# The modulated layer inside the recurrence's loop: four steps at a time, one body behind

## The reference

```python
x = x + lstm(x, h0=cond, Wx, Wh, b)      # x: (2, 1024, 256), cond: (2, 256)
x = x + modulated(x, cond, weight)       # weight: (256, 256)

def step(carry, xw_t):                   # 1024 times, one behind the other
    prev_h, prev_c = carry
    a = xw_t + prev_h @ Wh               # four gates of 256
    i, f, o = sigmoid(a[:, :256]), sigmoid(a[:, 256:512]), sigmoid(a[:, 512:768])
    g = tanh(a[:, 768:])
    next_c = f * prev_c + i * g
    next_h = o * tanh(next_c)
    return ((next_h, next_c), next_h)

ys = y * (1 / sqrt(256))                 # y: cond
d = rsqrt(einsum('bi,io->bo', ys * ys, weight * weight) + 1e-8)
out = einsum('bsi,io->bso', x * ys[:, None, :], weight) * d[:, None, :]
```

## Time and profile before

| | us |
|---|---|
| median of 3 runs | 1782.44 (1782.1 to 1782.82) |
| the profiled execution | 1781.28 |
| its span, first to last instruction | 1779.5 |
| PE busy | 1674.8 (94%) |
| PE weight loads busy | 1618.9 (91%) |
| ACT busy | 1096.3 (62%) |
| DVE busy | 1001.7 (56%) |
| POOL busy | 259.7 (15%) |
| mean granted TensorE clock | 0.993 of full |

### The profile page before, as it was taken

The page is one execution under the profiler, slowest core; times in us unless marked ns, Lnnn a source line. Parts: engine busy times, 40 slices in busy tenths (PEclk is TensorE's granted clock), DMA queues, the critical chain, the costliest instruction groups (busy, mean ns, idle before and its releaser), DMA issues.

```text
span 1779.5 us, 356718 instructions
## 1 busy us (share of the span) xinstructions
PE 1674.8 (94%) x164620; PEld 1618.9 (91%) x164620; DVE 1001.7 (56%) x7455; ACT 1096.3 (62%) x8196; POOL 259.7 (15%) x1293
## 2 busy tenths in 40 slices
PE   7999999999999999999999999999999999999998
PEld 6999999999999999999999999999999999999996
DVE  2555555555555555555555555555555555555554
ACT  2666666666666666666666666666666666666663
POOL 0111111111111111111111111111111111111110
PEclk7999999999999999999999999999999999999999
DMA  2000000000000000000000000000000000000001
GB/s 78 26 0 0 0 0 0 0 0 0 0 0 0 0 0 0 0 0 0 0 0 0 0 0 0 0 0 0 0 0 0 0 0 0 0 0 0 0 0 47
DMA packets 4585, 6.69 MB, mean 4 GB/s; under 512 B 1248, under 2 KB 3040, under 8 KB 4576
## 3 DMA queue, kind: packets, MB, share of 16 engines
q1 hardware_dynamic: 3872, 5.51, 0.9%
q10 hardware_dynamic: 704, 1.05, 0.2%
HBM read 4.46 MB, written 2.10 MB: 4 GB/s over the span
## 4 chain that ended last, share of the span: by engine, by line
PE 82%; DVE 12%; ACT 3%; issue 2%; DMA 0%; SPq 0%; POOL 0%; DVEq 0%
PE pG L228 32%; PE pX L210 18%; PE pH L228 14%; PE pS L228 14%; DVE pH L373 4%; DVE pH L349 4%; PE pF L241 3%; ACT fgate L186 3%; DVE hst L380 2%; DVE parts L368 2%; DVE pG L345 1%; PE pG L310 1%; DMA xh<-in_xT_dram 0%; PE pS L301 0%; DVE ores L397 0%
## 5 line engine op out<-in xcount | busy, mean ns | idle before, releaser
L228 PE MATMUL pG<-hst,wh_sb 128*32 128x16 f32 x65536 | 1081.6, 187 | 89.0 <-DVE hst L380 87.8
L228 PEld LDWEIGHTS pG<-hst,wh_sb 128*32 128x32 f32 x65536 | 943.4, 109 | 136.9 <-DVE hst L380 112.6
L186 ACT ACTIVATE fgate<-pH 128x2 f32<-128x2 f32 x2048 | 353.9, 173 | 601.0 <-PE pH L228 600.6
L228 PE MATMUL pH<-hst,wh_sb 128*32 128x16 f32 x32768 | 673.4, 185 | 3.5 <-issue 3.5
L368 DVE TENSOR_TENSOR parts<-fgate,pH 128x2 f32<-128x2 f32 x2048 | 320.3, 156 | 583.6 <-ACT fgate L186 583.4
L228 PEld LDWEIGHTS pH<-hst,wh_sb 128*32 128x32 f32 x32768 | 589.0, 110 | 2.1 <-issue 2.1
L228 PE MATMUL pS<-hst,wh_sb 128*32 128x16 f32 x32768 | 506.8, 186 | 3.4 <-issue 3.4
L210 PE MATMUL pX<-xp,wx_sb 128*32 128x8 f32 x32896 | 459.6, 181 | 2.9 <-issue 1.8
L228 PEld LDWEIGHTS pS<-hst,wh_sb 128*32 128x32 f32 x32768 | 424.4, 108 | 3.6 <-issue 3.6
L147 POOL TENSOR_TENSOR xh<-xh,hst 128x4 f32 (+1 forms) x1024 | 208.7, 204 | 1490.3 <-DVE hst L380 1490.3
L373 DVE TENSOR_TENSOR_SCAN pH<-parts 128x6 f32<-128x6 f32 x2048 | 367.2, 179 | 82.9 <-ACT parts L188 0.9
(11 more groups left out here) (41 smaller groups left out, 179.4 us busy)
## 6 DMA issues: line engine op xcount, KB each, us to landing
outT_dram<-ores SPq DMA_DIRECT2D x8, 256.0 KB, 2.5
xh<-in_xT_dram SPq DMA_DIRECT2D x6, 320.0 KB
wh_sb<-in_Wh_dram ACTq DMA_DIRECT2D x1, 1024.0 KB, 7.9
wx_sb<-in_Wx_dram SPq DMA_DIRECT2D x1, 1024.0 KB, 7.4
w_sb<-in_w_dram SPq DMA_DIRECT2D x1, 256.0 KB, 6.2
xh<-in_xT_dram SPq DMA_DIRECT2D x2, 64.0 KB, 8.0
condT<-in_condT_dram ACTq DMA_DIRECT2D x1, 2.0 KB, 7.6
bias_col<-in_bC_dram ACTq DMA_DIRECT2D x1, 3.0 KB, 7.3
```

The lines of the kernel that those rows point to most:

```text
L186: act.activation(fgate[:, j, :], forgets[j][:, cols], ACT.Sigmoid).then_inc(fgate_ready[j], 1)
L228: last = pe.matmul(to[c * Q:(c + 1) * Q, :], tile(wh_sb[:, k, :], c, j, g), hst[:, k, WIDE * t:WIDE * (t + 1)], start=False, stop=True, sk ...
```

## The change

The layer moves into the loop, one body behind the recurrence.

- POOL, once a body and behind the spread of x: `xm` = the body's four positions of `xh` times `yscale` (one buffer), and `res` += `xh` for the four positions that DVE has scaled. In front stand waits for its own adds, for PE's last layer sums (the buffer `xm` is read by them), and for DVE's last scaling. POOL also loads w itself, at the begin, and squares it in one instruction before the second spread.
- PE, in step 3 behind the output gate's matmuls: 16 matmuls (32 passes) of `w_sb` with `xm` into `pL`, a bank of its own in place of the filler's. The filler now goes into unused columns of the bank pX and stands before step 2's sums of x, not behind them.
- DVE, in step 0 between the multiply and the scan of half 0: `res` = `pL` times `demod`, at an address that depends on the counter.
- Before the loop: the sums for d on PE in 16 matmuls of 32 columns behind the warming ones and before the first sums of x, + eps on DVE, square root on ACT (its table is loaded first, the sigmoid's after it), reciprocal on DVE.
- SP sends `res` in three pieces, positions 0 to 511, 512 to 959, 960 to 1023, two DMAs each. All the work behind the loop but two scalings, two adds and one set of 16 matmuls is gone. `xh` and `res` begin with 8 columns of padding (X0), so that the first two sets, which hold nothing, have a place.

```diff
-    FILL = (0, 0, 1, 0)
+    X0 = 2 * T
+        xm = sb("xm", [P, K, ROWS])
+        res = sb("res", [P, K, B, X0 + SEQ])
-        wmod = sb("wmod", [P, B, K, D])
-        ores = sb("ores", [P, 2, NOUT])
-        pF = ctx.enter_context(nc.psum_tensor("pF", [P, 512], F32))
+        pL = ctx.enter_context(nc.psum_tensor("pL", [P, 512], F32))
...
+        OUTCUT = [0, 512, 960, SEQ]
@@ sync
+            for lo, hi in zip(OUTCUT, OUTCUT[1:]):
+                sp.wait_ge(result_ready, hi // T + 2)
+                for o in range(K):
+                    sp.dma_start(outT[o * P:(o + 1) * P, :, lo:hi], res[:, o, :, X0 + lo:X0 + hi]).then_inc(out_written, 16)
@@ gpsimd
+            pool.dma_start(w_sb[:, :, :], w.rearrange("(k p) o -> p k o", p=P)).then_inc(w_loaded, 16)
...
+            def add_x(n):
+                cols = bass.ds(n * T, T) if not isinstance(n, int) else slice(n * T, (n + 1) * T)
+                pool.tensor_tensor(res[:, :, :, cols], res[:, :, :, cols], xh[:, :, :, cols], ALU.add).then_inc(result_ready, 1)
             pool.wait_ge(x_begun, 16 * K)
-            spread(slice(0, T))
+            spread(slice(X0, X0 + T))
+            pool.wait_ge(w_loaded, 16)
+            pool.tensor_tensor(wsq[:, :, :], w_sb[:, :, :], w_sb[:, :, :], ALU.mult).then_inc(squares_ready, 1)
...
+                    pool.wait_ge(xh_ready, it * T + 2 * T)
+                    pool.wait_ge(layer_summed, it + 2)
+                    pool.wait_ge(layer_scaled, it + 1)
                     pool.wait_ge(x_summed, it + 2)
-                    spread(bass.ds(it * T + 2 * T, T))
+                    spread(bass.ds(it * T + (X0 + 2 * T), T))
+                    pool.tensor_tensor(xm[:, :, :].rearrange("p k (b t) -> p k b t", b=B), xh[:, :, :, bass.ds(it * T + X0, T)],
+                                       yscale[:, :, :].unsqueeze(3).broadcast_to([P, K, B, T]), ALU.mult).then_inc(xm_ready, 1)
+                    add_x(it)
@@ scalar
+            act.activation(warmed[:, 0:1], zeros[:, 0:1], ACT.Sqrt)
+            act.wait_ge(demod_added, 1)
+            act.activation(demod[:, :, :], demod[:, :, :], ACT.Sqrt).then_inc(demod_rooted, 1)
+            act.activation(warmed[:, 1:2], zeros[:, 0:1], ACT.Sigmoid)
@@ tensor
+            def sum_layer():
+                for o in range(K):
+                    for k in range(K):
+                        for c in range(G):
+                            lo = o * P + c * Q
+                            last = pe.matmul(layer[c * Q:(c + 1) * Q, o * ROWS:(o + 1) * ROWS], w_sb[:, k, lo:lo + Q], xm[:, k, :],
+                                             start=(o == 0 and k == 0), stop=True, skip_group_check=True)
+                return last
...
                     elif s == 2:
+                        filler(1)
                         sum_x_outs().then_inc(x_summed, 1)
                     else:
                         pe.wait_ge(xh_ready, it * T + (2 * T - 1))
-                    filler(FILL[s])
+                        pe.wait_ge(xm_ready, it + 1)
+                        sum_layer().then_inc(layer_summed, 1)
@@ vector
+            def scale_layer(n):
+                cols = bass.ds(n * T, T) if not isinstance(n, int) else slice(n * T, (n + 1) * T)
+                dve.wait_ge(layer_summed, n + 1)
+                dve.tensor_tensor(res[:, :, :, cols], layer.rearrange("p (o b t) -> p o b t", o=K, b=B),
+                                  demod[:, :, :].unsqueeze(3).broadcast_to([P, K, B, T]), ALU.mult).then_inc(layer_scaled, 1)
...
                         if s == T - 1:
                             carry_forget(j)
+                        elif s == 0 and j == 0:
+                            scale_layer(it)
                         dve.wait_ge(parts_ready[j], it * (2 * T) + 2 * (s + 1))
```

More of the change, by code:

```diff
@@ L52, in build @@
         zeros = sb("zeros", [P, P])
-        warmed = sb("warmed", [P, 1])
+        warmed = sb("warmed", [P, 2])
         condT = sb("condT", [P, K, B])
@@ L118, in _ @@
                 for k in range(K):
[L119 to L126, removed]
+                    sp.dma_start(xh[:, k, :, X0 + lo:X0 + hi], xT_in[k * P:(k + 1) * P, :, lo:hi]).then_inc(x_loaded, 16)
@@ L162, in _ @@
             pool.wait_ge(x_loaded, 16 * K * (len(XCUT) - 2))
[L163 to L169, removed]
+            bodies(EARLY, NBODY)
+            for n in (NBODY, NBODY + 1):
+                pool.wait_ge(layer_scaled, n + 1)
+                add_x(n)
         @block.scalar
@@ L236, in clear @@
                 for c in range(G):
-                    pe.matmul(of[c * Q:(c + 1) * Q, :], picks[:, :], zeros[:, 0:of.shape[1]], start=True, stop=True)
+                    last = pe.matmul(of[c * Q:(c + 1) * Q, :], picks[:, :], zeros[:, 0:of.shape[1]], start=True, stop=True)
+                return last
[6 more added lines that the diff above has]
+                                             start=(o == 0 and k == 0), stop=True, skip_group_check=True)
+                return last
             def filler(count, start=False):
                 for _ in range(count):
-                    pe.matmul(pF[0:Q, 0:P], picks[:, :], zeros[:, :], start=start, stop=True, skip_group_check=True)
+                    pe.matmul(pX[0:Q, 256:256 + P], picks[:, :], zeros[:, :], start=start, stop=True, skip_group_check=True)
             pe.wait_ge(zeros_ready, 1)
@@ L249, in _ @@
                 clear(outs[j])
+            clear(layer).then_inc(layer_summed, 1)
             filler(WARM, True)
+            pe.wait_ge(squares_ready, 1)
+            pe.wait_ge(ysq_ready, 1)
+            for o in range(K):
+                for k in range(K):
+                    for c in range(G):
+                        lo = o * P + c * Q
+                        last = pe.matmul(squared[c * Q:(c + 1) * Q, o * B:(o + 1) * B], wsq[:, k, lo:lo + Q], ysq[:, k, :],
+                                         start=(o == 0 and k == 0), stop=True, skip_group_check=True)
+            last.then_inc(demod_summed, 1)
             pe.wait_ge(operands_ready, 2)
@@ L293, in _ @@
                         pe.wait_ge(xh_ready, it * T + (2 * T - 1))
-                    filler(FILL[s])
-            pe.wait_ge(squares_ready, K)
-            pe.wait_ge(outs_carried, NBODY + 1)
-            pe.wait_ge(h_ready[0], SEQ + 1)
-            for o in range(K):
-                for k in range(K):
-                    last = pe.matmul(pD[:, o * B:(o + 1) * B], wsq[:, k, o * P:(o + 1) * P], ysq[:, k, :],
-                                     start=(k == 0), stop=(k == K - 1))
-            last.then_inc(demod_summed, 1)
-            pe.wait_ge(wmod_ready, B * K)
-            pe.wait_ge(xh_ready, T + SEQ)
-            for n, (b, ch, o) in enumerate(UNITS):
-                if n >= 2:
-                    pe.wait_ge(result_ready, n - 1)
-                for k in range(K):
-                    last = pe.matmul(pO[n % 2][:, :], wmod[:, b, k, o * P:(o + 1) * P],
-                                     xh[:, k, b, ch * NOUT:(ch + 1) * NOUT], start=(k == 0), stop=(k == K - 1))
-                last.then_inc(layer_summed, 1)
+                        pe.wait_ge(xm_ready, it + 1)
+                        sum_layer().then_inc(layer_summed, 1)
+            pe.wait_ge(layer_scaled, NBODY + 1)
+            pe.wait_ge(xm_ready, NBODY + 1)
+            sum_layer().then_inc(layer_summed, 1)
         @block.vector
@@ L342, in _ @@
                 dve.tensor_copy(hst[:, j, h_slot(0):h_slot(0) + B], condT[:, j, :]).then_inc(h_ready[j], 1)
+            dve.wait_ge(demod_summed, 1)
+            dve.tensor_scalar(demod[:, :, :], squared.rearrange("p (o b) -> p o b", o=K), EPS, None, ALU.add).then_inc(demod_added, 1)
             def carry_pair(j):
@@ L384, in _ @@
                         carry_outs()
[L386 to L399 removed]
+            for n in (NBODY, NBODY + 1):
+                scale_layer(n)
 def kernel(**inputs):
```

62 lines of the change are left out of this document (23 added, 39 removed).

## The result

| | before | after |
|---|---|---|
| median of the runs, us | 1782.56 (1782.1 to 1782.82) | 1852.34 (1850.8 to 1852.49) |
| span of the profiled execution, us | 1779.5 | 1850.5 |
| mean granted TensorE clock | 0.993 | 0.994 |
| PE busy | 94% | 97% |

What follows compares the result with a forecast made beforehand. The recurrence PE to ScalarE to VectorE and back was taken as the bound. About 0.32 us per body times 256 is 81; 1781.3 + 81 + 2 - 13.3 = 1851, median 1852, range 1806 to 1888.

Steps and rivals of the forecast that it cites:

- PE's step 3: Loop's end on PE: the layer's 32 passes and waits delay the branch and next body by 0.22 us per body.
- the room: PE's back edge: of 0.44 us idle, the branch needs 0.34 to 0.39, leaving 0.05 to 0.10 free.
- DVE's step 0: Between multiply and first scan: scaling's register instructions delay the scan 0.10 us per body (0.04 to 0.18, or nothing).
- PE's step 2: Filler moves ahead of the output gate's sums of x; last load comes 0 to 0.03 us late, 0.01 taken.
- start: Before the loop: loading and squaring w and PE's demodulation passes, partly offset by earlier instruction stops, add 2 us (0 to 4).
- tail: From the last h to the end: 5.5 us instead of 18.8, a gain of 13.3 us.
- body: One loop pass of four steps: about 7.1 us expected, against 6.76 before.
- the 1.2 added for the median: Whole kernel: median of the runs lies 1.2 us above the profiled execution, taking 1851 to 1852.
- The rival in which PE's sequencer hides the branch by running ahead of the array: PE's back edge: sequencer over about 0.25 us ahead, both prices hidden, kernel faster at 1771 us; chance 0.09.
- One sign of being right: Step 3's end: some 0.3 us idle between last pL load and next body's first load, put down to issue, not h.
- The late copy: POOL's copy of x for PE comes some 0.35 us later; hidden, but up to 0.05 per body without the late edge.

Runs made afterwards that it cites:

- 32 dummy passes: Kernel before plus 16 matmuls (32 passes of zeros into a spare bank) at the end of step 3: 1832.27 us, ratio 1.029.
- 8 passes: Kernel before plus 4 matmuls (8 passes of zeros into a spare bank) at the end of step 3: 1781.64 us, ratio 0.9997.
- cut layer: Changed kernel with 16 of the layer's passes in step 2 in the filler's place and 16 in step 3: 1809.31 us, ratio 1.0163.
- copy first: Changed kernel with POOL's copy of x ahead of its other waits, and add of x and modulation swapped: 1856.08 us, ratio 1.0418.
- the kernel with half a layer: Changed kernel with only the first 128 outputs in the loop (16 passes in step 2), DVE's scaling behind h's second half, the rest behind the loop: 1786.12 us.
- late scaling: Changed kernel with DVE's scaling of the layer moved behind h's second half in step 0: 1833.25 us, ratio 1.0298.
- late scaling and cut layer: Changed kernel with scaling behind h's second half in step 0 and the layer's passes half in step 2, half in step 3: 1795.74 us, ratio 1.0079.
- the two parts alone: Kernel before with 32 zero passes in PE's step 3 (1832.27 us), and separately with a waiting, counted-address operation in DVE's step 0 (1809.72 us).

## Why the prediction was right

The mechanism came out, both prices on the loop within their bounds:

| term | predicted | measured |
|---|---|---|
| PE's step 3, per body | 0.22 (0.10 to 0.30) | 0.21; 0.19 by 32 dummy passes on the kernel before |
| of that, the room that takes off | 0.05 to 0.10 | 0.04 |
| DVE's step 0, per body | 0.10 (0 to 0.18) | 0.11 in the step; 0.12 from multiply to scan |
| PE's step 2, per body | 0.01 (0 to 0.03) | 0.00 |
| start | +2 (0 to 4) | +0.3 by this pair of traces; about +1.9 over all |
| tail | -13.3 | -13.4 |
| body | about 7.1 | 7.10 |

That the sum met 1852.34 to the microsecond is luck. The loop lost 84 us and not 81, the start of this trace took 1.7 less than forecast, and the 1.2 added for the median was not there (the profiled execution took 1852.27): +3, -1.7 and -1.2 cancel.

**PE's edge.** That the idle 0.44 before a body's first load was the branch and little room had been read from one place, the first back edge. The two runs with dummy passes show it: 8 passes fit, 32 do not. The traces give its price. In each kernel whose branch is the last to come, the next body's first load starts 0.36 us behind the start of the branch's row (the median; 0.41 in up to two bodies of ten), so step 3 is as long as the branch's start says. Medians of 230 bodies, in us from the start of step 3:

| kernel | branch's row starts | plus 0.36 | step 3 |
|---|---|---|---|
| before | 1.29 | 1.65 | 1.69, h comes last |
| 8 passes | 1.31 | 1.67 | 1.69, h comes last |
| cut layer, 16 passes | 1.36 | 1.72 | 1.72 |
| 32 dummy passes | 1.52 | 1.88 | 1.88 |
| changed kernel | 1.54 | 1.90 | 1.90 |
| changed, copy first | 1.57 | 1.93 | 1.93 |

The room was 0.04 (1.69 less 1.65), just under the 0.05 to 0.10 of the prediction, and the layer put the branch back by 0.25. The rival in which PE's sequencer hides the branch by running ahead of the array falls with it. A small part of it is true: in the changed kernel the branch starts 0.12 before the last load's end, in the kernel before 0.05 behind it, which is why the loads rest 0.24 and not 0.34 to 0.39. One sign of being right failed in name only: the loads' idle was to be put down to issue, and is still put down to h.

**DVE's scan.** The counted address and the wait cost 0.12, in the middle of the bounds, and the operation itself nothing. The carry of the kernel before, which has neither, rightly showed that the operation would be free; it could not show that the scaling would be.

**POOL.** The late copy was said to be hidden, up to 0.05 per body without the late edge. It came 0.20 later (0.35 had been said) and was hidden (copy first gave the changed kernel nothing), and it did come out as soon as PE was on time: 0.03 in the kernel with half a layer, gone when POOL's order changed. What the prediction left out is the other way in which POOL's work reaches the loop, by making DVE's scans longer: some 2 us of the changed kernel (0.008 a body), the 0.04 of step 0 with the late scaling, and the 0.05 of step 1 with late scaling and cut layer.

**The start.** In the pair of traces the loop is entered 2.0 us later (15.06 for 13.05), as forecast, but the second body begins only 0.33 later, because PE's stops in the first body are shorter (0.80 for the first shown against 1.96, 1.41 for the last against 1.60). These stops differ from trace to trace, though. In the five kernels with the old start (two of them clear one bank more) the second body begins at 29.7, 31.4, 31.6, 32.2 and 32.2, in the six with the new one at 32.6, 32.9, 33.1, 33.2, 33.9 and 34.1. The means are 1.9 apart, and that is the forecast; the 0.3 of the one pair is not a measure of the term.

**What stays open.** By their traces the two parts alone make the loop 51.2 and 28.9 us longer, 80 of the 84. Most of the other 4 stands in step 3, whose mean is 1.908 with the layer and 1.893 with the dummy passes, and which has one wait more; that the wait is the reason was not tried. The long scans add some 2 in step 0. The counted address and the wait on DVE were not taken apart. And the kernel with the copy first has a step 3 longer by 0.02, for a reason that no run isolates.

## What to carry to other kernels

Idle time ahead of a loop's first instruction belongs to the branch until it is shown otherwise: look for a back edge at which the data had come early, and count only what is left as room. An operation inserted into a recurrence is priced by its register instructions before its own length; put the one with a counted address where its engine waits for nobody. When work is moved under a recurrence, measure the room of each step (here 48 passes in step 2, 8 in step 3) and move only as much as fits, even if that is half. An engine off the recurrence can still reach it by lengthening an instruction on it: compare the length of the same instruction with and without the neighbour's work beside it.

## What the runs showed of the hardware

- From the start of a taken branch's row on PE to the next body's first load passed 0.36 us in the median of each of the kernels in which the branch came last, although the row shows 208 ns and the register instruction's 44. From the last load's end it was 0.24 (changed kernel) to 0.31 (32 dummy passes, cut layer).
- On DVE an operation of 0.17 us between two that depend on each other cost nothing (0.19 from one to the other with and without it), while the same with a counted address and a wait made it 0.31.
- 16 passes in step 3 cost 0.03 and 32 cost 0.21: behind the edge of the room the further 16 cost 0.18, 0.011 us each, with one wait more in front of them. The 32 loads shown start within 0.27 (0.38 less one load of 0.11), 0.009 each.
- PE's stops in the first body are not a fixed price. Those over 0.7 us add up to 9.2 us in the trace of the kernel before and to 7.3 in the changed one's; in four further kernels with the old start to 6.4, 8.7, 8.9 and 9.0.
- A scan on DVE took 0.18 us, and up to 0.26 in the changed kernel's loop, when a two-input operation of POOL ran beside it; beside POOL's copy alone it took 0.18 each of 456 times.
